# Cross-attention: GpSimd adds the two halves of each head's exponentials, VectorE sums 39 partial values per head in place of 77

## The reference, cut to what matters

```python
def cross_attention(x, ctx, wq, wk, wv, wo, bo):
    q = einsum('bne,ef->bnf', x, wq)      # 20 heads of 64
    k = einsum('bme,ef->bmf', ctx, wk)    # M = 77
    v = einsum('bme,ef->bmf', ctx, wv)
    scores = einsum('bhnd,bhmd->bhnm', q, k) * SCALE
    attn = softmax(scores, axis=-1)       # over the 77 context rows
    out = einsum('bhnm,bhmd->bhnd', attn, v)
    return einsum('bnf,fe->bne', out, wo) + bo
```

## Time and profile before

| | us |
|---|---|
| median of 3 runs | 1015.6 |
| profiled execution, its own time | 1019.83 |
| span of the profiled execution | 1018.0 |
| busy: TensorE (matmul) | 974.7 |
| busy: VectorE | 683.6 |
| busy: ScalarE | 588.9 |
| busy: GpSimd | 377.5 |
| L1770 VectorE sums, 32 instructions | 30.2 |
| L1843 GpSimd scaling, 32 instructions | 48.2 |

### The profile page before, as it was taken

One profiled execution on the slowest core, in us unless ns is written; L12 is line 12 of the kernel. 1 busy time (PEld: TensorE's weight loads), 2 busy tenths in 40 slices (PEclk: granted clock), 3 DMA queues, 4 the chain that ended last, 5 costly groups with the idle time before them and its releaser, 6 DMA issues.

```text
span 1018.0 us, 17405 instructions
## 1 busy us (share of the span) xinstructions
PE 974.7 (96%) x6346; PEld 700.8 (69%) x6346; DVE 683.6 (67%) x1164; ACT 588.9 (58%) x1326; POOL 377.5 (37%) x486
## 2 busy tenths in 40 slices
PE   7999989999999999999999999999999989999998
PEld 3566665666567666567666567666566689998887
DVE  3666737776674776674776674776636879999463
ACT  3665636666764666764666764666735455445442
POOL 3576714443332443332444332434311034444120
PEclk9999999999999999999999999999999999999999
DMA  9310230000000000000000000000001330000000
GB/s 268 102 42 2 55 96 1 1 2 1 1 2 1 1 1 2 1 1 1 1 1 1 2 1 2 1 1 1 2 1 36 104 83 1 1 2 1 2 27 26
DMA packets 19585, 22.18 MB, mean 22 GB/s; under 512 B 1366, under 2 KB 17070, under 8 KB 19502
## 3 DMA queue, kind: packets, MB, share of 16 engines
q1 hardware_dynamic: 19502, 21.09, 7.3%
HBM read 15.83 MB, written 1.31 MB: 17 GB/s over the span
## 4 chain that ended last, share of the span: by engine, by line
PE 66%; DVE 10%; ACT 4%; issue 4%; POOL 1%; DMA 0%; SPq 0%; DVEq 0%; ACTq 0%; POOLq 0%
PE banks L413 13%; PE banks L400 12%; PE banks L386 11%; PE banks L420 4%; PE banks L228 3%; ACT sa_probs L503 3%; PE banks L1626 3%; PE banks L229 2%; PE banks L231 2%; PE banks L230 2%; PE banks L1918 2%; DVE ca_top L1761 2%; PE banks L236 2%; DVE ca_probs L1766 2%; DVE sa_negmax L575 1%
## 5 line engine op out<-in xcount | busy, mean ns | idle before, releaser
L647 POOL TENSOR_SCALAR sa_probs<-sa_probs,sa_inverse 128x512 f32<-128x512 f32 x320 | 217.7, 696 | 362.6 <-DVE sa_inverse L579 362.5
L503 ACT ACTIVATE sa_probs<-banks,sa_negmax 128x512 f32<-128x512 f32 x320 | 215.9, 686 | 125.7 <-DVE sa_negmax L575 125.6
L575 DVE TENSOR_REDUCE sa_negmax<-banks 128x2 f32<-128x1024 f32 x160 | 188.7, 1218 | 10.3 <-PE banks L386 7.3
L400 PEld LDWEIGHTS banks<-ident,sa_probs 128*128 128x128 f32 x1280 | 144.4, 140 | 55.6 <-issue 27.6
L400 PE MATMUL banks<-ident,sa_probs 128*128 128x128 f32 x1280 | 172.5, 275 | 10.0 <-ACT sa_turned L514 5.6
L584 DVE COPY sa_turned<-banks 128x512 f32<-128x512 f32 x160 | 110.2, 688 | 75.3 <-PE banks L400 75.3
L413 PE MATMUL banks<-sa_turned,sa_v 128*64 128x512 f32 x640 | 155.0, 605 | 0.0
L386 PE MATMUL banks<-sa_k_parts,sa_q_parts 64*128 64x512 f32 x960 | 133.1, 408 | 1.9 <-ACT sa_probs L503 1.9
L514 ACT COPY sa_turned<-banks 128x512 f32<-128x512 f32 x160 | 94.3, 589 | 58.1 <-PE banks L400 56.3
L386 PEld LDWEIGHTS banks<-sa_k_parts,sa_q_parts 64*128 64x128 f32 x960 | 84.0, 184 | 30.4 <-issue 14.1
L413 PEld LDWEIGHTS banks<-sa_turned,sa_v 128*64 128x64 f32 x640 | 38.7, 136 | 74.2 <-issue 73.0
(11 more groups left out here) (205 smaller groups left out, 1701.9 us busy)
## 6 DMA issues: line engine op xcount, KB each, us to landing
ad_x_t<-in_x_turned SPq DMA_DIRECT2D x4, 512.0 KB, 5.0
ad_x_pad<-in_x_padded SPq DMA_DIRECT2D x4, 512.0 KB, 8.8
w_o<-in_L_xattn_wo SPq DMA_DIRECT2D x2, 800.0 KB, 9.0
x<-in_x SPq DMA_DIRECT2D x1, 1280.0 KB, 9.1
out<-x SPq DMA_DIRECT2D x4, 320.0 KB, 2.4
w_q_t<-in_L_xattn_wq_t SPq DMA_DIRECT2D x1, 1120.0 KB, 10.6
fold_values<-ca_turned SPq DMA_DIRECT2D x5, 192.5 KB
fold_values<-ca_probs SPq DMA_DIRECT2D x4, 192.5 KB
```

Of the source, the lines that this page charges most:

```text
L400: last = pe.transpose(b_turn[e][:, q * P:(q + 1) * P], probs[:, j % 2, e, q, k * P:(k + 1) * P], ident[:])
L503: act.activation(probs[:, j % 2, e, q, :], b_scores[u % 2][:, e, :], ACT.Exp, bias=negmax[:, u % RING, e:e + 1], accum_out=total[:, u % RI ...
L575: dve.tensor_reduce(negmax[:, u % RING, :], b_scores[u % 2], AX_X, ALU.max, negate=True).then_inc(s_max.sem, 1)
L647: pool.tensor_scalar(probs[:, j % 2, e, q, :], probs[:, j % 2, e, q, :], inverse[:, u % RING, e:e + 1], 1.0, ALU.mult, ALU.mult).then_inc( ...
```

## The change

Ahead of each `invert`, GpSimd runs `add_halves`: it adds the first 38 exponentials of each of the 10 heads to the next 38 (380 values written) and copies the 77th of each head beside them (10 values). VectorE then sums 39 partial values for each head instead of 77 exponentials. The partial values lie in unused columns of the tile `w_q_t`, one buffer for each half u. VectorE's sum waits for GpSimd's copy instead of ScalarE's exponential; GpSimd's addition waits for the exponential and for the sum that read the buffer one tile before. Nothing on TensorE, ScalarE or the DMA queues changes.

```diff
+        SUMS = SK // 2 + 1
+        partial = wq_t[:].rearrange("p j d -> p (j d)")[:, INNER:INNER + 2 * HH * SUMS].rearrange("p (u h k) -> p u h k", u=2, h=HH)
...
-        s_sum = sig("sum_made", 2)
+        s_part = sig("partial_sums_made", 4)
+        s_sum = sig("sum_made", 2, 2)
...
             def invert(t, u):
-                dve.wait_ge(s_exp.sem, s_exp.at(t, u))
-                dve.tensor_reduce(total[:, t % RING, u, :], probs[:, t % RING, u, :, :], AX_X, ALU.add).then_inc(s_sum.sem, 1)
+                dve.wait_ge(s_part.sem, s_part.at(t, 2 * u + 1))
+                dve.tensor_reduce(total[:, t % RING, u, :], partial[:, u, :, :], AX_X, ALU.add).then_inc(s_sum.sem, 1)
...
+            def add_halves(t, u):
+                p, half_keys = probs[:, t % RING, u, :, :], SUMS - 1
+                pool.wait_ge(s_exp.sem, s_exp.at(t, u))
+                pool.wait_ge(s_sum.sem, s_sum.at(t - 1, u))
+                pool.tensor_tensor(partial[:, u, :, 0:half_keys], p[:, :, 0:half_keys], p[:, :, half_keys:2 * half_keys], ALU.add).then_inc(s_part.sem, 1)
+                pool.tensor_copy(partial[:, u, :, half_keys:SUMS], p[:, :, 2 * half_keys:SK]).then_inc(s_part.sem, 1)
...
             for u in range(2):
+                add_halves(0, u)
                 scale(0, u)
+            add_halves(1, 0)
             scale(1, 0)
...
                 if t + 1 < NT:
+                    add_halves(t + 1, 1)
                     scale(t + 1, 1)
                 if t + 2 < NT:
+                    add_halves(t + 2, 0)
                     scale(t + 2, 0)
```

More of the change, by code:

```diff
@@ L1745, in _ @@
         def _(dve):
-            for s in (s_v, s_lo, s_sub, s_x):
+            for s in (s_v, s_lo, s_sub, s_sum, s_x):
                 dve.sem_inc(s.sem, s.credit)
```

## The result

| | before | changed |
|---|---|---|
| median of 5 runs, us | 1015.6 (1014.93 to 1016.07) | 1021.73 (1020.1 to 1022.08) |
| ratio to before, 95% interval | | 1.0055 [1.0042, 1.0069] |
| span of the profiled execution | 1018.0 | 1020.3 |
| busy: VectorE / GpSimd | 683.6 / 377.5 | 674.4 / 410.9 |
| GpSimd's wait for the reciprocal in the stage | 101.4 | 42.8 |

The change costs 6.1 us. The two spans are only 2.3 apart: the profiled execution of before lay 4.2 above its median and had two stretches of lower granted clock in this stage.

A forecast was written before the change was run, and what follows sets the result against it. VectorE was taken to pace the stage, TensorE close behind, with a new VectorE-GpSimd ring costing time. First tiles +2.3, three rounds +3.9 and end -0.4 gave +5.8 on 1015.6: 1021.4 us, range 1015.5 to 1024.5.

The forecast's parts named there:

- The ring: Reciprocal, scaling, addition, copy, next sum across VectorE and GpSimd: 3.04 us, so VectorE waits 0.86; as pacesetter, chance 0.64.
- rival 2: The ring binds at the cheap rate: addition 0.82, copy 0.04, ring 2.77; 1016.1 us, no change; chance 0.16.
- The removed work: VectorE's sum over 390 instead of 770 values: start of sum to reciprocal 0.60 instead of 0.98, 0.38 us less.
- The halves where the saving stays: Sums behind the low parts of x and the normalized x (L157): VectorE's way outlasts the ring, -0.38 us each.
- The absorbed waits: VectorE's waits for TensorE's scores, about 0.7 us a round, vanish because VectorE now comes later.
- The round: Four tiles, 33.6 us before: +2.01 from the halves less about 0.7 of waits, +1.3 to 34.9; three give +3.9.
- The first tiles: Start of the stage, where sums follow closely: second reciprocal +3.4, TensorE's first product +2.7, +2.3 us where the rounds begin.
- The end: Behind sum(14, 0): one more sum with the low parts of x in front saves 0.38 us, entered as -0.4.
- The sum, +5.8: Whole kernel: first tiles 2.3, rounds 3.9, end -0.4, added to the median of 1015.6 for 1021.4 us.
- Signs named ahead: Changed profile: VectorE waits for the copy, none behind L218 and L157; rounds 34.9; TensorE idles over 2 us; first product about 823.
- Rival 4: VectorE and GpSimd block each other: L218 waits for the addition, 1.13 us at four places, 1025.9; chance 0.12 with other losses.
- Rival 3: TensorE becomes the bound if addition and copy take under about 0.3 us: rounds 32.6, total 1011.6 us; chance 0.08.

The follow-up runs named there:

- Dead additions: The change with GpSimd still adding and copying, but VectorE summing all 77 exponentials without waiting for them; 1017.97 us, ratio 1.0012.
- normalization alone: The change without the one addition that meets L157 (tiles 4, 8, 12, half 1, summed in full); 1021.27 us, ratio 1.005.
- before again: The kernel before, unchanged, measured and profiled a second time; 1015.16 us, ratio 0.9992.
- No copy: The change without the copy of the 77th exponential, which is left out of the sum; 1017.57 us, ratio 1.0028.
- Late additions: The change with tiles 0 and 1 summed in full and without their additions; 1019.46 us, ratio 1.0051.
- change again: The changed kernel, unchanged, measured and profiled a second time; 1021.26 us, ratio 1.0052.
- short sum: The kernel before with its sum over only 39 of the 77 exponentials and no additions; 1010.17 us, ratio 0.9944.
- Addition twice: The change with each addition run a second time behind the first, VectorE waiting for the copy behind both; 1044.45 us, ratio 1.0303.
- half 1 ahead: The change with partial sums only for half 1 from tile 1 on, each addition ahead of half 0's scaling; 1016.17 us, ratio 1.0004.

## Why the prediction was right, and where not

The forecast of 1021.4 us against 1021.73 holds, and the mechanism named first is there: a ring in which the scaling stands between the reciprocal and the next addition. That the total came so close is in part luck. By the terms below, as an estimate, the ring net of the saved time accounts for about 3 us (0.32 in each round and 1.9 in the first tiles), the meeting with L157, which the prediction did not have, for 1.6, and TensorE's low clock in the first tiles for 0.7.

- **The ring, 3.04 us: 2.89.** The addition holds the ring for 0.82 (one alone lasts 0.87), not 0.99; the two-operand rate from the earlier trace rows priced it too high. Net of the fixed 0.18 the addition runs at 0.69 / 380 = 1.8 ns a value, nearer the scaling's rate. The row of 320 values, 0.862, is only 0.01 shorter than this one of 380; it writes another type (fp32r), and why it costs more a value was not tested. The Trainium skill's rate for two inputs (GPSIMD Engine Reference, "Performance versus the Vector engine"), 2.6 cycles at 1.2 GHz, gives 1.00 by the same sum, as an estimate; the 0.87 of the trace lies below it. Copy and handover took 0.24 for 0.19, with 0.03 from the end of the copy to the sum. VectorE waits 0.62 at a second sum, not 0.86. By this alone the second sums, the statistics and the weights were priced 0.15 to 0.17 too high each, 0.95 a round. By the prediction's own sign ("it is mis-sized if the addition runs at 0.82 or below") this term stands at the edge: 2.89 lies between its 3.04 and the 2.77 of rival 2, nearer to the latter. What rival 2 had too low was the copy, at 0.04.
- **The removed work, 0.38 a sum.** Right: start to reciprocal is 0.60 (873.39 to 873.99).
- **The halves where the saving stays.** Behind the low parts of x it did: 5.13 for 5.15. Behind L157 it did not: 4.90 was predicted, 5.43 measured. This is the step of the sum that failed: "The same behind the normalized x (879.32 to 883.62, 4.30): -0.38." It left the time of L157 as it was. Dead additions show the cause without any wait for the sum, 2.96 for 2.38; normalization alone takes it away again.
- **The absorbed waits, 0.7.** Right: they stood in the two halves of 3.50 and 3.57 in before again, and the change has 3.48 in all four.
- **The round, +1.3: +0.85.** The two errors have opposite signs: -0.95 and +0.53. With the ring as measured and L157 unchanged, the prediction's own sum would have given about +0.35 a round. Three rounds give +2.55, not +3.9.
- **The first tiles, +2.3: +2.64.** Part of it is TensorE's low clock. No copy, with a ring only 0.16 shorter and the clock at 1.00, took 1.48 more than before again; dead additions, with no ring but one stretch at 0.50, took 0.72 more. So about 0.7 is the clock, as an estimate from these two, and the ring alone gives near 1.9. Late additions, with neither ring nor low clock there, took 20.33. The first product came at 821.65, which is 3.1 later against the stage's start than in before again, for +2.7.
- **The end, -0.4: -0.08.** The one half behind the low parts of x saved its 0.39 (5.14 for 5.53), but the two halves behind it took 0.78 more, so that VectorE's last reciprocal came 0.39 later. TensorE's slack covered that, and the saving did not arrive.
- **The sum, +5.8.** The pair profiled again gives +5.1 in the stage; the medians of the same two runs are 6.1 apart. The total was right partly because the rounds were priced too high and the first tiles too low, and 1.0 of the 6.1 stands in no profile.
- **Signs named ahead.** Waits of VectorE in front of its sums were there, none behind L218 and L157. Rounds are 34.48 apart, not 34.9. The first product was expected near 823 and came at 821.65 in change again, whose stage started 1.8 earlier than that of the profile that the prediction read. TensorE's idle time did not show: the waits in the round of change again are 0.9 us in front of L1617 and 0.2 of L1629, while its busy time rose from 32.60 to 33.41 for the same 230 matmuls. The waits too short to appear stand in the records of the matmuls, which is an inference.
- **Rival 4, 1025.9.** Its mechanism exists, in another place. L218 kept its 1.85; beside it the addition stretched to 1.31. L157, which the rival did not name, paid 0.53 a round. It was at work before the change too: L218 takes 0.68 in the stages where GpSimd does nothing, and 1.85 here (last section).
- **Rival 3** has a measured floor now: 32.19 a round, 1010.17 in all, in short sum. The floor is lower than the 32.6 at which the prediction had TensorE stop the rounds.

Open: in which executions the clock falls in the first tiles or at the end. Addition twice, late additions and before itself show the lower clock at the end, the other runs do not, and no difference in the order of their work was found that would sort them. A start of the stage that differs by up to 2.3 us between executions (804.9 to 807.2) stays open too.

## What to carry to other kernels

An engine with idle time helps only if its instructions can stand between the moments at which others wait for it: write down the ring from one result through its in-order queue to the next, and compare its length with what covers it now. Then look at what the added instructions run beside: here VectorE and GpSimd made each other wait where no semaphore joins them. And place an offload only in those halves where the relieved engine is behind. Here one addition of eight, the one behind the low parts of x, brought the 0.4 us a round of the fastest kernel that still sums all 77 values, as its halves show. A second and a third each shortened a half, and VectorE lost the same time again in the next one, waiting for TensorE's scores.

## What the runs showed of the hardware

**VectorE and GpSimd take turns.** Short rows of the changed kernel, L157's durations (ns min/median/max) and first and last start over two rounds:

```profile
L157 DVE TENSOR_SCALAR ln_hat<-x,ln_moments,ln_rstd x8: 314/626/1610, 847.9 to 884.9; 128x160 f32<-128x160 f32 x8
```

and of normalization alone:

```profile
L157 DVE TENSOR_SCALAR ln_hat<-x,ln_moments,ln_rstd x8: 314/353/1612, 848.1 to 884.4; 128x160 f32<-128x160 f32 x8
```

Undisturbed, one of the four instructions takes 0.31 to 0.35. The longest, 1.61, is the one that meets the scaling of 1.48; with the addition queued behind the scaling a second one is lengthened, to 0.90, and the median rises from 353 to 626. With two additions (addition twice) three are, and the median is 962. So the scaling and each addition that run beside these four hold up one of them each; beside the copy of 0.22 none was longer. For a single long instruction it is the other way: L218 has its turn behind the scaling, and the addition waits. Timeline of the changed kernel, GpSimd beside L218 (866.17 to 868.02):

```profile
865.77 1.71 POOL L1853 TENSOR_TENSOR ca_probs<-ca_probs,ca_inverse 128x770 f32<-128x770 f32 x1 [1.02 <-DVE ca_inverse L1775]
867.44 1.31 POOL L1846 TENSOR_TENSOR w_q_t<-ca_probs 128x380 f32<-128x380 f32 x1
868.70 0.20 POOL L1847 COPY w_q_t<-ca_probs 128x10 f32<-128x10 f32 x1
```

The addition is 0.44 longer than its usual 0.87, and ends 0.7 behind L218.

The kernel before paid for such meetings already. Timeline of VectorE in before, L218 where GpSimd does nothing and in the second round of this stage, beside the scaling:

```profile
139.83 0.68 DVE L218 TENSOR_TENSOR ln_y_tail<-ln_full_tail,ln_y_tail 32x512 fp32r<-32x512 f32 x1
...
863.62 1.85 DVE L218 TENSOR_TENSOR ln_y_tail<-ln_full_tail,ln_y_tail 32x512 fp32r<-32x512 f32 x1
```

and of VectorE in normalization alone, in the one round in which L275 started 0.09 ahead of the scaling (which then took 1.73) and not behind it:

```profile
891.59 0.48 DVE L275 TENSOR_TENSOR wb_tail<-w_k,wb_tail 32x320 fp32r<-32x320 f32 x1
```

So 1.17 us of each L218 and of each L275 (0.48 for 1.65), and 1.26 of L157 (0.35 for 1.61), are spent beside the scaling, in the rounds of before as in those of the change.

The Trainium skill (SBUF — State Buffer, "Who interferes with whom") says that whichever of the two issues first has the shared port pair for its whole instruction, and that the other is blocked until then. These rows agree, and add that the turn goes over after each instruction. Which of the two was first, the recorded starts do not tell within 0.07 us: in half 1 ahead the addition started 0.07 ahead of L216 each time, and in the first round it was the addition that grew (1.43), in the others L216 (1.35).

**The granted clock.** In change again TensorE's granted clock went to 0.50, the 1.2 GHz level, about an idle time of 2.44 us in the first tiles; in dead additions it did so (0.50 from 817 to 820) behind one of 0.91, and in no copy it stayed at the upper level behind 2.12. The length of one idle time alone does not decide it in these runs. A profiled execution should be read for its clock by stretches before its span is compared: the first profile of before was 4.2 us above its median, and its first tiles and its end, where the clock was low, are 1.7 us longer each than in before again (22.50 for 20.79, and 20.54 for 18.88).
